# Start-up of a fused conditioning and feed-forward kernel: GpSimd's weight squares behind x, banks of their own for the first group, a finer split of the up matrix, and block 1 conditioned a chunk later

## The reference, cut to what matters

```python
h   = einsum('bct,bcd->bdt', x, weights[cond])     # conditioning: 128 rows, each with its own 32x32 matrix
s   = square(relu(h @ up_w)) @ down_w              # 256 -> 1024 -> 256
moe = (h @ expert_w) * sum(top_k(h @ gate_w, 2))
y   = s + moe
out = x + layernorm(y) * gamma + beta
```

## Time and profile before

| | |
|---|---|
| median of 3 runs | 229.41 us |
| the profiled execution | 229.29 us |
| its span in the trace | 227.6 us |
| PE busy | 220.9 us (97%) |
| DVE busy | 160.9 us (71%) |
| GpSimd busy | 131.4 us (58%) |
| ACT busy | 106.4 us (47%) |
| mean granted TensorE clock | 0.998 |

### The profile page before, as it was taken

How to read it: one execution, slowest core, us unless ns; L and a number is a source line. 1 busy time by engine, 2 the same in 40 slices (tenths; PEclk the granted TensorE clock), 3 DMA queues, 4 the chain that set the end, 5 groups by cost and what they waited for, 6 DMA issues and landing times.

```text
span 227.6 us, 3998 instructions
## 1 busy us (share of the span) xinstructions
PE 220.9 (97%) x1260; PEld 191.4 (84%) x1260; DVE 160.9 (71%) x352; ACT 106.4 (47%) x187; POOL 131.4 (58%) x131
## 2 busy tenths in 40 slices
PE   7899999999999999999999999999999999999992
PEld 2798888888888889888889888888888888888892
DVE  6587965777667777667667766577766766777885
ACT  3379865444555345534545444544454444444000
POOL 3758795665545763656455764366555575557411
PEclk9999999999999999999999999999999999999999
DMA  3877123030603010000200002000020002000031
GB/s 98 231 213 230 50 59 103 10 98 7 187 10 98 9 66 30 0 0 3 92 0 0 3 0 95 3 0 0 0 95 1 0 0 68 28 0 0 10 108 69
DMA packets 17177, 11.81 MB, mean 52 GB/s; under 512 B 6660, under 2 KB 16900, under 8 KB 17156
## 3 DMA queue, kind: packets, MB, share of 16 engines
q1 hardware_dynamic: 15460, 10.43, 15.1%
q10 hardware_dynamic: 1280, 1.07, 1.4%
q0 software_dynamic: 416, 0.05, 0.2%
HBM read 7.35 MB, written 4.19 MB: 51 GB/s over the span
## 4 chain that ended last, share of the span: by engine, by line
PE 94%; DMA 1%; issue 1%; DVE 1%; ACTq 1%; POOLq 0%; POOL 0%; ACT 0%; DVEq 0%
PE up_ps L337 39%; PE down_ps L431 25%; PE down_ps L433 13%; PE hid_ps L303 5%; PE moe_ps L449 3%; PE moe_ps L448 3%; PE moe_ps L447 3%; DMA wd<-in_L_cond_weights_dram 1%; PE down_ps L303 1%; ACTq L513 1%; DMA cond_row<-in_itok_B_dram 1%; POOLq L46 0%; POOL rstd L697 0%; DVE result L615 0%; DVE stats L588 0%
## 5 line engine op out<-in xcount | busy, mean ns | idle before, releaser
L682 POOL TENSOR_TENSOR sq_lo<-square,sq_hi 128x512 fp32r<-128x512 f32 x64 | 84.4, 1322 | 77.0 <-DVE square L553 77.0
L431 PE MATMUL down_ps<-down_hl,sq_hi 128*128 128x512 f32 x248 | 88.8, 393 | 0.0
L553 DVE SCALAR_TENSOR_TENSOR square<-up_ps,relu 128x512 f32<-128x512 f32 x64 | 44.0, 687 | 37.3 <-ACT relu L491 28.2
L433 PE MATMUL down_ps<-down_hl,sq_lo 128*128 128x256 f32 x248 | 69.6, 280 | 0.0
L431 PEld LDWEIGHTS down_ps<-down_hl,sq_hi 128*128 128x128 f32 x248 | 46.5, 188 | 10.8 <-issue 0.3
L491 ACT ACTIVATE relu<-up_ps 128x512 f32<-128x512 f32 x64 | 38.2, 596 | 35.8 <-PE up_ps L337 35.7
L337 PE MATMUL up_ps<-hid_hi,up_hi 128*128 128x512 f32 (+1 forms) x136 | 52.8, 391 | 0.3 <-ACT hid_hi L476 0.3
L337 PE MATMUL up_ps<-hid_hi,up_lo 128*128 128x512 f32 (+1 forms) x136 | 51.1, 379 | 0.0
L433 PEld LDWEIGHTS down_ps<-down_hl,sq_lo 128*128 128x128 f32 x248 | 46.7, 188 | 2.4
L493 ACT ACTIVATE sq_hi<-relu 128x512 fp32r<-128x512 f32 x64 | 40.6, 634 | 2.0
L337 PE MATMUL up_ps<-hid_lo,up_hi 128*128 128x512 f32 (+1 forms) x136 | 40.6, 381 | 0.0
(11 more groups left out here) (62 smaller groups left out, 193.3 us busy)
## 6 DMA issues: line engine op xcount, KB each, us to landing
x_sb<-in_x_dram SPq DMA_DIRECT2D x7, 512.0 KB, 4.2
out_dram<-result SPq DMA_DIRECT2D x7, 512.0 KB, 3.0
wd<-in_L_cond_weights_dram SPq DMA_DIRECT2D x111, 4.0 KB, 1.5
x_sb<-in_L_ffn_down_w_dram SPq DMA_DIRECT2D x2, 512.0 KB, 4.7
x_sb<-in_x_dram ACTq DMA_DIRECT2D x2, 256.0 KB, 2.9
result<-in_L_ffn_up_w_dram ACTq DMA_DIRECT2D x2, 256.0 KB, 2.9
result<-in_L_ffn_up_w_dram SPq DMA_DIRECT2D x1, 512.0 KB, 4.7
out_dram<-result SPq DMA_DIRECT2D x4, 128.0 KB, 1.7
```

Of the source, the lines that this page charges most:

```text
L431: pe.matmul(dst[:, :], a_hi, down_hl[:, c, :, :].rearrange("p s t -> p (s t)"), start=(c == 0), stop=False)
L433: mm = pe.matmul(dst[:, T:2 * T], a_lo, down_hl[:, c, 0, :], start=False, stop=(c == CH - 1))
L553: dve.scalar_tensor_tensor(square[:, c % 2, :], up_ps[c % UPB][:, :], 0.0, relu[:, c % 2, :], ALU.max, ALU.mult).then_inc(square_done, 1)
L682: pool.tensor_tensor(sq_lo[:, j % 2, c, :], square[:, c % 2, :], sq_hi[:, j % 2, c, :].bitcast(f32), ALU.subtract).then_inc(sq_lo_done, 1)
```

## The change

The squares 8, 9, 10 and 12 are GpSimd's now and 11, 13, 14 and 15 SP's; GpSimd first waits for the first half of x, and groups 2 and 3 have semaphores of their own. The first half's two groups are conditioned as parts 0 and 1: group 0 into `up_ps[2]` and `up_ps[3]`, group 1 into `hid_ps` and `moe_ps`, each copied and subtracted at 128 columns. Chunks 4 to 7 of the up matrix are still one load, but are rounded and subtracted as 4 and 5 ahead of block 0's first square, and 6 and 7 after it: their rounding between `square(0)` and `eg_lo`, their subtraction after `square(1)`. Block 1 is conditioned at c=5.

```diff
-UP_SPLITS = [slice(0, 2), slice(2, 4), slice(4, CH)]
+UP_LOADS = [slice(0, 2), slice(2, 4), slice(4, CH)]
+UP_SPLITS = [slice(0, 2), slice(2, 4), slice(4, 6), slice(6, CH)]
-BY_SP, BY_ACT, BY_POOL, BY_SP_LATER = (0, 2, 4, 6), (1, 3, 5, 7), (8, 9, 10, 11, 12), (13, 14, 15)
+BY_SP, BY_ACT, BY_POOL, BY_SP_LATER = (0, 2, 4, 6), (1, 3, 5, 7), (8, 9, 10, 12), (11, 13, 14, 15)
...
         def rounds_at(j, c):
-            return {4: (0, 1)}.get(c, ()) if j == 0 else {2: (0,), 4: (1,)}.get(c, ())
+            return {5: (0, 1)}.get(c, ()) if j == 0 else {2: (0,), 4: (1,)}.get(c, ())
...
-        def first_bank(half, k):
-            return ((hid_ps, moe_ps), down_ps)[half][k]
+        def first_bank(part, k):
+            return (up_ps[2:4], (hid_ps, moe_ps), down_ps)[part][k]
+        def part_tok(part):
+            return (slice(0, P), slice(P, HALF_TOK), slice(HALF_TOK, TOK))[part]
...
         (PE, conditioning_first)
                     pe.wait_ge(wd_first_landed[0], 16 * Q)
-                    condition(0, 0, 0)
-                    condition(0, 1, 0)
+                    condition(0, 0, 0).then_inc(hid_done, 1)
+                    condition(0, 1, 0).then_inc(hid_done, 1)
...
-                    pe.wait_ge(wd_later_landed[0], 16 * len(BY_SP_LATER))
-                    pe.wait_ge(wd_later_landed[1], 16 * len(BY_POOL))
-                    for k in range(K):
-                        condition(0, k, 2)
-                        condition(0, k, 3).then_inc(hid_done, 1)
+                    later_landed(2)
+                    condition(0, 0, 2)
+                    condition(0, 1, 2)
+                    later_landed(3)
+                    condition(0, 0, 3).then_inc(hid_done, 1)
+                    condition(0, 1, 3).then_inc(hid_done, 1)
...
         (PE, first_rounded)
                     up_ready(c, up_hi_ready)
+                    if c in (2, 3):
+                        pe.wait_ge(hid_lo_done, c - 1)
...
         (ACT, and DVE likewise)
-            hidden_first(0, 0)
-            hidden_first(0, 1)
+            for part in range(2):
+                hidden_first(part, 0)
+                hidden_first(part, 1)
             split_up(1)
-            hidden_first(1, 0)
-            hidden_first(1, 1)
+            hidden_first(2, 0)
+            hidden_first(2, 1)
...
         (DVE)
             dve.wait_ge(up_landed[2], 16)
-            dve.tensor_copy(up_hi[:, :, split_cols(2)], up_raw[:, :, split_cols(2)]).then_inc(up_hi_ready, 1)
+            round_up(2)
             split_up(2)
...
                     if j == 0 and c == 0:
+                        round_up(3)
                         dve.wait_ge(eg_hi_ready, 1)
                         dve.tensor_tensor(eg_lo[:, :, :], eg_raw[:, :, :], eg_hi[:, :, :].bitcast(f32), ALU.subtract) \
                             .then_inc(eg_lo_ready, 1)
+                    if j == 0 and c == 1:
+                        split_up(3)
...
         (GpSimd)
+            pool.wait_ge(x_first_landed[0], 16)
             pool.wait_ge(cond_first_landed, 16)
             values = conditions(mybir.EngineType.Pool, range(HALF_BLOCK, 2 * HALF_BLOCK))
             pool.wait_ge(wd_zeroed[0], 1)
             for b in BY_POOL:
-                pool.dma_start(square_of(b), weights_of(values[b])).then_inc(wd_later_landed[1], 16)
+                pool.dma_start(square_of(b), weights_of(values[b])).then_inc(wd_later_by_pool[b // Q], 16)
```

More of the change, by code:

```diff
@@ L109, in adaln_ffn @@
         x_landed = {j: sem(f"x_landed{j}") for j in range(1, BLOCKS)}
-        up_landed = [sem(f"up_landed{n}") for n in range(len(UP_SPLITS))]
+        up_landed = [sem(f"up_landed{n}") for n in range(len(UP_LOADS))]
         down_landed = [sem(f"down_landed{n}") for n in range(DOWN_LOADS)]
@@ L115, in adaln_ffn @@
         wd_first_landed = [sem(f"wd_first_landed_group{g}") for g in range(TILES // 2)]
-        wd_later_landed = [sem("wd_later_landed_sp"), sem("wd_later_landed_pool")]
+        wd_later_by_sp = {g: sem(f"wd_later_landed_group{g}_sp") for g in range(TILES // 2, TILES)}
+        wd_later_by_pool = {g: sem(f"wd_later_landed_group{g}_pool") for g in range(TILES // 2, TILES)}
         wd_second_landed = [sem("wd_second_landed_sp"), sem("wd_second_landed_pool")]
@@ L173, in rounds @@
         def rounds(j, k):
-            return K * (j + 1) + k + 1
+            return K * (j + 2) + k + 1
         def experts_at(j, c):
@@ L220, in weights_of, with load_up @@
             return cond_w[bass.ds(row, 1), :, :].rearrange("s c d -> (s c) d")
-        def load_up(queue, part):
-            cols = split_cols(part)
-            queue.dma_start(up_raw[:, :, cols], up_rows[:, :, cols]).then_inc(up_landed[part], 16)
+        def load_up(queue, load):
+            cols = slice(P * UP_LOADS[load].start, P * UP_LOADS[load].stop)
+            queue.dma_start(up_raw[:, :, cols], up_rows[:, :, cols]).then_inc(up_landed[load], 16)
         def load_x_first(queue, half):
@@ L248, in _ @@
             for b in BY_SP_LATER:
-                sp.dma_start(square_of(b), weights_of(values[b])).then_inc(wd_later_landed[0], 16)
+                sp.dma_start(square_of(b), weights_of(values[b])).then_inc(wd_later_by_sp[b // Q], 16)
             load_up(sp, 2)
@@ L299, in condition @@
                 if j == 0:
-                    dst = first_bank(t // 2, k)[:, P * (t % 2):P * (t % 2) + P]
+                    dst = first_bank(min(t, 2), k)[:, P * (t // 3):P * (t // 3) + P]
                 else:
@@ L303, in condition, with later_landed @@
                 return pe.matmul(dst, x_sb[:, g, P * k:P * k + P], wd[:, g, :], start=True, stop=True)
+            def later_landed(g):
+                pe.wait_ge(wd_later_by_sp[g], 16 * sum(b // Q == g for b in BY_SP_LATER))
+                pe.wait_ge(wd_later_by_pool[g], 16 * sum(b // Q == g for b in BY_POOL))
             def conditioning_first(half):
@@ L348, in first_rounded @@
                     up_ready(c, up_hi_ready)
+                    if c in (2, 3):
+                        pe.wait_ge(hid_lo_done, c - 1)
                 if c == 0:
-                    pe.wait_ge(hid_hi_done, K * half + 1)
+                    pe.wait_ge(hid_hi_done, K * (half + 1) + 1)
                 up_product(0, c, half_tok(half), up_hi, 0, hid_hi, 0)
@@ L355, in first_rounded @@
                 if c == 0:
-                    pe.wait_ge(hid_hi_done, K * half + 2)
+                    pe.wait_ge(hid_hi_done, K * (half + 1) + 2)
                 up_product(0, c, half_tok(half), up_hi, 1, hid_hi, 2)
@@ L362, in first_rest @@
                 if c == 0:
-                    pe.wait_ge(hid_lo_done, K * half + 1)
+                    pe.wait_ge(hid_lo_done, K * (half + 1) + 1)
                 up_product(0, c, half_tok(half), up_hi, 0, hid_lo, 4)
                 if c == 0:
-                    pe.wait_ge(hid_lo_done, K * half + 2)
+                    pe.wait_ge(hid_lo_done, K * (half + 1) + 2)
                 return up_product(0, c, half_tok(half), up_hi, 1, hid_lo, 5)
@@ L472, in hidden, with hidden_first @@
                 act.activation(hid_hi[:, j % 2, k, :], round_bank(j, k)[:, :], ACT.Copy).then_inc(hid_hi_done, 1)
-            def hidden_first(half, k):
-                act.wait_ge(hid_done, K * half + k + 1)
-                act.activation(hid_hi[:, 0, k, half_tok(half)], first_bank(half, k)[:, 0:HALF_TOK], ACT.Copy) \
+            def hidden_first(part, k):
+                tok = part_tok(part)
+                act.wait_ge(hid_done, K * part + k + 1)
+                act.activation(hid_hi[:, 0, k, tok], first_bank(part, k)[:, 0:tok.stop - tok.start], ACT.Copy) \
                     .then_inc(hid_hi_done, 1)
@@ L541, in hidden, with hidden_first @@
                                   hid_hi[:, j % 2, k, :].bitcast(f32), ALU.subtract).then_inc(hid_lo_done, 1)
[L543 to L546, removed]
+            def hidden_first(part, k):
+                tok = part_tok(part)
+                dve.wait_ge(hid_hi_done, K * part + k + 1)
+                dve.tensor_tensor(hid_lo[:, 0, k, tok], first_bank(part, k)[:, 0:tok.stop - tok.start],
+                                  hid_hi[:, 0, k, tok].bitcast(f32), ALU.subtract).then_inc(hid_lo_done, 1)
             def square_up(j, c):
@@ L621, in split_up, with round_up @@
                                   up_hi[:, :, split_cols(part)].bitcast(f32), ALU.subtract).then_inc(up_lo_ready, 1)
+            def round_up(part):
+                dve.tensor_copy(up_hi[:, :, split_cols(part)], up_raw[:, :, split_cols(part)]).then_inc(up_hi_ready, 1)
             def split_down(part):
```

## The result

The changed kernel takes 230.24 us, the median of 11 runs (230.17 to 230.59); the kernel before, timed beside it, 229.41 (11 runs, 229.17 to 230.07). The ratio is 1.0033, with a 95% interval of 1.0024 to 1.0042: 0.83 us slower by the medians. The profiled execution took 230.28 us with a span of 228.7, against 229.29 and 227.6. The forecast was 230.7, slower, with a range of 229.4 to 231.9.

A forecast was written before the change was run, and what follows sets the result against it. PE's full queue from its first up matmul was taken as the bound: 229.29 - 0.10 (first group's banks) + 0.3 (wait for squares) + 1.2 (late chain to block 1's hid_lo) = 230.7 us, range 229.4 to 231.9.

The forecast's parts named there:

- The bound: From the first up matmul at 7.74 us PE is a full queue; any new wait goes to the end one for one.
- The first group's banks: At PE's start: copying group 1 at 128 columns instead of 256 starts PE at 7.64, winning 0.10 us.
- The bound by the second up load: At chunk 2: its subtraction ends at 9.22, its matmul starts at 9.35, so at most about 0.13 us is won.
- the prediction's own signs of being wrong: No PE wait at block 1's first hid_lo, eg_lo taking 0.7 us, or PE's first up matmul before 7.5.
- The squares of groups 2 and 3: Near 10 us: GpSimd's later squares make group 3 land at 10.4, asked for at 10.1; PE waits 0.3 us more.
- Up in two and block 1 later: From first square to 25 us: sq_lo(0) precedes eg_lo, block 1's hid_lo come late, PE stands 1.2 us later.
- the prediction's lower bound: At block 1's hid_lo near 25 us: if eg_lo gets in first, the late chain costs only 0.2 us.
- The squares didn't land later than taken: Rival, chance 0.20: group 3 lands at 11.1, PE waits 1.0 us; 231.4, or 231.9 with up's load later too.
- The chain didn't stay in time: Rival, chance 0.24: eg_lo goes ahead of sq_lo(0) or shutting out costs less; 229.7, or 229.4 without group 3's wait.
- The third rival: Chance 0.06, faster: without GpSimd's squares beside them, group 1's last square and second up load land 0.3 us earlier; 228.8.
- a rule of full exclusion: Near 14 us: DVE's fast copies also lock out GpSimd, so round_up(3) delays GpSimd's start by some 0.15 us.

The follow-up runs named there:

- e5: Changed kernel with block 1 conditioned back at c=4 and up's second half rounded and subtracted whole: 229.52 us, ratio 0.9999.
- e6: Kernel before with only the first group's own banks added (squares shared as before, no wait for x): 229.43 us, ratio 0.9992.
- e10: e9 with the second up load (chunks 2 and 3) rounded and subtracted one chunk at a time: 229.66 us, ratio 0.9997.
- e2: Changed kernel with block 1 conditioned back at c=4, the finer split of up kept: 229.92 us, ratio 1.0013.
- e3: Changed kernel with up's second half rounded and subtracted whole again, ahead of the first square: 229.54 us, ratio 0.9994.
- e1: Kernel before with one edit, block 1 conditioned at c=5: 229.81 us, ratio 1.0007.
- e4: Changed kernel with GpSimd's first sq_lo made to wait until eg_lo is done: 230.22 us, ratio 1.0025.
- e7: Changed kernel without GpSimd's wait for the first half of x: 230.32 us, ratio 1.0033.
- e12: e3 with the second up load in two and GpSimd's sq_lo(5) waiting for DVE's subtraction of down's second part: 229.59 us, ratio 0.9999.
- e8: Changed kernel with ACT and DVE taking block 1's hi and lo parts ahead of down's second part: 230.42 us, ratio 1.0039.
- e11: e5 with the second up load rounded and subtracted one chunk at a time: 229.51 us, ratio 0.9996.
- e9: e3 with block 1's hi and lo parts taken ahead of down's second part, as in e8: 230.01 us, ratio 1.0016.

## Why the prediction was right, point by point

**The bound** was named rightly: PE's queue, and what is lost on the way to 26 us goes to the end (1.04 us at 25.90, 1.1 in the span).

**The first group's banks** (forecast 0.10 won, bounds 0 and 0.13). ACT's copy of 128 columns took 0.28, as worked out. PE started at 7.48, 0.26 earlier: the copy's 0.10, and 0.15 by which the copy began earlier (7.06, was 7.21), behind a square that landed 0.4 earlier. At chunk 2 nothing of it was left: the matmul with chunk 2's lo part is at 9.32 (before 9.35), but the one behind it at 9.55 (9.49), and group 2 is conditioned at 9.79 (9.73), 0.06 later. So this term was 0.10 too good and is zero at best. The bound by the second up load, given as a limit of the gain, was the term itself. e5, e6 and e10 show it.

One of the prediction's own signs of being wrong appeared here: a first up matmul before 7.5. It came at 7.48, because the sum held the landing of group 1's last square for fixed. That it missed the limit by only 0.02 is luck: in the ten profiles of kernels with the wait for x it came at 7.36 to 7.52 in six and at 7.80 to 7.82 in four. The other two signs, no wait at `hid_lo` and an `eg_lo` of 0.7 us, didn't appear.

**The squares of groups 2 and 3** (forecast 0.3 waited, bounds 0 and 1.0). GpSimd's first issue is at 5.38 (forecast 5.35), the last at 7.1. It took 2.9 us to land where I took 3.3, so group 3 was there at 10.0 and PE, held at chunk 2 before, didn't wait: 0. This is the term that was most too large. The rest of the difference is in the next. SP's later issues cost nothing here, as forecast, but not by cover alone: the load of chunks 4 to 7 was issued at 7.50 instead of 7.01 and landed after 3.9 us instead of 4.7, so at 11.4 instead of 11.7.

**Up in two and block 1 later** (forecast 1.2). The order is as forecast link by link: `sq_lo(0)` at 14.04 (14.05), `eg_lo` until 15.95 (16.05), the fifth square at 19.64 (19.7), down's subtraction until 24.3 (24.5), the `hid_lo` at 24.9 and 25.5 (25.2 and 25.8), PE 1.04 later (1.2). The prediction takes the two parts as one chain, and the runs bear that out: with the conditioning late, the finer split costs 230.24 - 229.54 = 0.7 (0.86 when each is held against the kernel before beside it), with the conditioning early 0.35 (e2). The late conditioning costs nothing without the split (e3, and e1's 0.24 is inside its interval; PE's wait of 0.21 in e1 is the 0.2 that the prediction's lower bound has for an `eg_lo` that gets in first). That the wait at the experts lies within this and is not added is shown by e4.

**The sum** was 229.29 - 0.10 + 0.3 + 1.2 = 230.7; measured in the profiled executions it is 229.29 + 1.04 = 230.33, and 230.28 was taken. The 1.04 is all that PE has lost by 25.90, the start's 0.06 included. The forecast is 0.4 too high: 0.3 for squares that PE didn't wait for and 0.16 too much for the chain, against 0.10 of gain that didn't come.

**The rivals.** The squares didn't land later than taken. The chain didn't stay in time. The third rival's mechanism is real (e7: 0.3 us earlier landings without GpSimd beside), and I was wrong to say that the wait for x shields nothing; but it needed the second up load to come earlier too, and that was issued at 5.05 and took 2.8 us, as before.

## What to carry to other kernels

When an engine that seems to have slack is given one more instruction, or another order, look for what it shares with its neighbour: here a DVE subtraction of two SBUF tiles and a GpSimd one didn't advance together in any meeting that was read, and the DVE one, when it came second, took 1.4 to 1.8 us instead of 0.7 (a `sq_lo` that came second 1.70 instead of 1.27). An earlier first step can then make the whole chain later, because it lets the other engine in first. And where a tuned order has its slack spread over several consumers, undoing one wait shows the next one within half a microsecond (`hid_lo`, then the experts of tile 2), so the gain of a start that is 0.25 us earlier is to be followed to the first thing that didn't move with it, here a load that lands at 7.9 us.

## What I had not expected of the hardware

The shutting out follows GpSimd's instruction as it is moved: `eg_lo` 1.54 us with `sq_lo(0)` ahead, 0.71 with it behind (e4), and the same for down's second part, 1.43 and 0.69 (e3, e12). DVE's squares, which read PSUM and SBUF, took 0.67 to 0.69 throughout, all 64 of them, beside `sq_lo` too. The rounding of chunks 6 and 7 (13.81 to 14.23) overlapped the start of `sq_lo(0)` (14.04), which took 1.35 instead of the 1.27 to 1.31 of others, so 0.04 to 0.08 us was lost there rather than the 0.15 that I had given for a rule of full exclusion.

Two things at the start vary from one execution to the next. The ten warm-up matmuls took between 3.80 (e6) and 4.45 us (the changed kernel) in the profiles. In the changed kernel they start (5.45 - 1.64) / 9 = 0.42 us apart; 512 columns in that time are 1.2 per ns, the lower of the clock's two levels (later 0.233, 2.2 per ns), while the row of the granted clock says 1.00. In the profiles of e3, e7, e8, e11 and e12 group 1's conditioning behind them was slow too: 0.59 to 0.64 us for its first two matmuls instead of 0.39 to 0.49. In these five PE's first up matmul came at 7.80 to 7.89.

And the spread of the times: the kernel before spreads over 0.9 us in its 11 runs (229.17 to 230.07), the changed one over 0.4. The second up load, which holds PE until 9.3 us, isn't the reason, since e5 has it too and spreads over 0.68. Kernels in which PE waits again for DVE's chain, past 16 us (e2, e4, e7, e8, e9), spread over 0.10 to 0.28, which would fit a wait that swallows what the start varies by; but the changed kernel, which has that wait, spreads over 0.42, and e6, which hasn't, over 0.38. The cause stays open.
